# Attention and expert feed-forward on one core: output weights prepared earlier, four output tiles projected inside the last head pair

## The reference

```
x = L0_attn_x                                   # [2, 2048, 1024] f32
x = x + layernorm(attn(layernorm(x)))           # 16 heads of 64, causal, with biases
x = x + layernorm(ffn(layernorm(x)))

attn(x): q, k, v = x @ w.T + b; softmax(q k^T / 8, causal) v; @ wo.T + bo

ffn(x):  per expert n of 8:
    x_diff = x - select_mean_diff[n];  x_diff /= norm(x_diff)
    score[n] = sum_s (select_weight[n, :, s] . x_diff) ** 2
    gate[n] = sigmoid(imp_slope[n] * (score[n] - imp_center[n]))
  scale = max gate, i = argmax gate
  mod = bias_w[i] + lora_degen[i] . (lora_update[i] . (x - debias_w[i]))
  return (1 - scale) * x + scale * mod
```

## Time and profile before

| | us |
|---|---|
| three runs | 2406.46, 2402.87, 2405.65 |
| median | 2405.65 |
| span of the profiled execution | 2400.4 |
| time of the profiled execution | not given apart; the median stands 5.25 above the span |
| PE busy | 2271.6 |
| DVE, ACT, POOL busy | 1675.7, 1741.4, 1633.9 |

### The profile page before, as it was taken

The page is one execution under the profiler, slowest core; times in us unless marked ns, Lnnn a source line. Parts: engine busy times, 40 slices in busy tenths (PEclk is TensorE's granted clock), DMA queues, the critical chain, the costliest instruction groups (busy, mean ns, idle before and its releaser), DMA issues. The chain is left out here.

```text
span 2400.4 us, 70752 instructions
## 1 busy us (share of the span) xinstructions
PE 2271.6 (95%) x28666; PEld 1448.5 (60%) x28666; DVE 1675.7 (70%) x4148; ACT 1741.4 (73%) x2380; POOL 1633.9 (68%) x1291
## 2 busy tenths in 40 slices
PE   6999999999999998899999999999999679999996
PEld 4566667575757655557575757575766445455453
DVE  8487777777777766566666666666676846777777
ACT  6577777877777766677777777777787846666665
POOL 3588888888888876678788888888898822222221
PEclk9999999999999999999999999999999889999998
DMA  8699999999999999999999999999999986656662
GB/s 244 124 196 202 194 211 207 196 203 204 209 197 197 208 200 198 198 200 193 174 195 181 189 183 187 185 184 185 182 192 195 232 169 155 165 153 174 149 168 79
DMA packets 1414420, 447.44 MB, mean 186 GB/s; under 512 B 1391664, under 2 KB 1392064, under 8 KB 1414096
## 3 DMA queue, kind: packets, MB, share of 16 engines
q1 hardware_dynamic: 1414096, 442.92, 99.7%
HBM read 67.95 MB, written 41.94 MB: 46 GB/s over the span
## 5 line engine op out<-in xcount | busy, mean ns | idle before, releaser
L1051 POOL TENSOR_TENSOR hl<-probs,hl 128x1024 f16<-128x1024 f32 x544 | 1166.6, 2151 | 350.2 <-ACT hl L903 348.1
L896 ACT ACTIVATE probs<-s_ps,exp_bias 128x1024 f32<-128x1024 f32 (+7 forms) x768 | 633.3, 854 | 316.5 <-DVE exp_bias L730 309.7
L725 DVE TENSOR_REDUCE neg_max<-s_ps 128x1 f32<-128x1024 f32 (+7 forms) x768 | 675.8, 904 | 169.2 <-PE s_ps L526 169.1
L903 ACT ACTIVATE hl<-probs 128x1024 f16<-128x1024 f32 x544 | 575.0, 1057 | 90.2 <-DMA pt<-hl 74.1
L549 PE MATMUL o_ps<-v,pt 128*128 128x65 f16 x4352 | 431.1, 193 | 50.2 <-DMA pt<-hl 43.8
L549 PEld LDWEIGHTS o_ps<-v,pt 128*128 128x128 f16 x4352 | 400.5, 96 | 79.3 <-DMA pt<-hl 36.9
L526 PE MATMUL s_ps<-nat 64*128 64x512 f16 (+3 forms) x3840 | 410.1, 351 | 25.9 <-ACT probs L896 22.4
L550 PE MATMUL o_ps<-v,pt 128*128 128x65 f16 x4352 | 431.4, 194 | 0.0
L551 PE MATMUL o_ps<-v,pt 128*128 128x65 f16 x4352 | 430.2, 192 | 0.0
L550 PEld LDWEIGHTS o_ps<-v,pt 128*128 128x128 f16 x4352 | 399.8, 97 | 19.1
L551 PEld LDWEIGHTS o_ps<-v,pt 128*128 128x128 f16 x4352 | 400.3, 98 | 0.0
(11 more groups left out here) (185 smaller groups left out, 3580.9 us busy)
## 6 DMA issues: line engine op xcount, KB each, us to landing
w_raw<-in_w_pairs SPq DMA_DIRECT2D x48, 576.0 KB, 4.8
o_scratch<-o_hl SPq DMA_DIRECT2D x128, 128.0 KB, 2.6
out<-result SPq DMA_DIRECT2D x31, 512.0 KB, 3.1
x_in<-in_x SPq DMA_DIRECT2D x27, 512.0 KB, 4.9
pt<-hl SPq DMA_TRANSPOSE x544, 5.2
xn_scratch<-xn SPq DMA_DIRECT2D x16, 512.0 KB, 3.8
xn<-in_x SPq DMA_DIRECT2D x11, 512.0 KB, 3.8
x_in_c<-in_x SPq DMA_DIRECT2D x10, 512.0 KB, 3.9
```

Of the source, the lines that this page charges most:

```text
L725: nc.vector.tensor_reduce(neg_max[:, step.round, acc, h:h + 1], s_ps[(n + h) % S_RING][:, first:end], AX_X, ALU.max, negate=True).then_inc ...
L896: last = nc.scalar.activation(probs_of(n)[:, cols], s_ps[n % S_RING][:, cols], ACT.Exp, bias=exp_bias[:, step.round, acc, h:h + 1], scale= ...
L903: nc.scalar.activation(hl_of(n, 0), probs_of(n), ACT.Copy).then_inc(p_hi_done, 1)
L1051: nc.gpsimd.tensor_tensor(hl_of(n, 1), probs_of(n), hl_of(n, 0), ALU.subtract).then_inc(p_lo_done, 1)
```

## The change

Four things are changed.

1. The splitting of w_o moves out of the last pair. From step 8 of pair 8 to pair 12 one block per 8 steps (`wo_block`) is loaded into x_in (part 0), summed on ACT (1), centred on DVE (2), its high part made on ACT (3), its low part on DVE (4), and stored from xn to a new DRAM scratch (5). Both buffers are those of the norm, which is over after pair 6. In the last pair SP loads the eight finished blocks (512 KB each) into the arena in its steps 3 to 6, two per step. POOL has no part in it any more.
2. In the last pair's steps 9 to 16 PE projects one half of tiles 0 to 3 per step into u_ps, between scores and times_v (`project_early`), and DVE copies it out in the next step (`early_out`). Six `load_o` stand in SP's steps 5, 7, 9, 10, 12 and 14, the last three behind a wait for proj_done. After the last pair PE projects tile 4 instead of tile 0.
3. The last stage has six attn buffers instead of two. Its 54 halves that are left are laid out by `project_at`: steps 1 to 31 have two halves each, and steps 2, 5, ..., 23 only one. So the projection is four tiles ahead at first and back at the old place from step 24. The other work keeps its step.
4. Row loads, other loads and `center_rows` of the last pair come up to three steps earlier. nat[0] lies in the new tile attn_first.

```diff
+FIRST_WO = HALF_PAIRS * NSTEP + 8
+WO_SPAN = 8
+def wo_block(p, i, part):
+    k, at = divmod(p * NSTEP + i - FIRST_WO, WO_SPAN)
+    return k if 0 <= k < KT and at == part else None
+EARLY_TILES, EARLY_FIRST = 4, 9
+EARLY_HALVES = 2 * EARLY_TILES
...
@@ SP, body of a pair
-                    if kind == "last" and i == NSTEP - LAG:
-                        fin["load_o"](sp, 0)
-                        fin["load_x"](sp, 0)
...
-                            sp.dma_start(wo_raw[k], fin["w_view"][k]).then_inc(wo_loaded[k], 16)
...
+                    k = wo_block(p, i, 0)
+                    if k is not None:
+                        if k:
+                            sp.wait_ge(wo_lo_done, k)
+                        else:
+                            sp.wait_ge(xn_lo_done, 2 * LN_TILES)
+                        sp.dma_start(x_in[:], fin["w_view"][k]).then_inc(wo_loaded, 16)
+                    k = wo_block(p, i, 5)
+                    if k is not None:
+                        sp.wait_ge(wo_lo_done, k + 1)
+                        sp.dma_start(wo_scratch[k], xn[:]).then_inc(wo_stored, 16)
+                    if kind == "last" and 3 <= i < 3 + KT // 2:
+                        if i == 3:
+                            sp.wait_ge(unit_done, N_UNIT * PAIRS)
+                            sp.wait_ge(wo_stored, 16 * KT)
+                        for k in (2 * (i - 3), 2 * (i - 3) + 1):
+                            sp.dma_start(fin["w_pair"][:, :, k, :], wo_scratch[k].rearrange("p (l d) -> p l d", l=2)).then_inc(
+                                wo_ready[k], 16)
...
+                    if kind == "last":
+                        for tile, at in enumerate((5, 7, 9, 10, 12, 14)):
+                            if i == at:
+                                if tile >= 3:
+                                    sp.wait_ge(fin["proj_done"], 2 * (tile - 3) + 2)
+                                fin["load_o"](sp, tile)
+                        if i in (13, 15):
+                            fin["load_x"](sp, (i - 13) // 2)
@@ PE
+            def project_early(n):
+                m, h = divmod(n, 2)
+                if h == 0:
+                    pe.wait_ge(fin["ot_loaded"][m % 3], 16 * (m // 3 + 1))
+                if n == 0:
+                    pe.wait_ge(full_done, N_UNIT * PAIRS)
+                    for k in range(KT):
+                        pe.wait_ge(wo_ready[k], 16)
+                else:
+                    pe.wait_ge(fin["attn_done"], n)
+                project_half(nc, fin, m, h, u_ps[:])
...
+                    if kind == "last" and i >= EARLY_FIRST:
+                        project_early(i - EARLY_FIRST)
@@ DVE
+            def early_out(n):
+                m, h = divmod(n, 2)
+                dve.wait_ge(fin["proj_done"], n + 1)
+                dve.wait_ge(fin_centered, 1)
...
+                    if kind == "last" and i > EARLY_FIRST:
+                        early_out(i - EARLY_FIRST - 1)
@@ last stage
+ONE_HALF = range(2, 25, 3)
+def project_at():
+    halves, at = [divmod(n, 2) for n in range(EARLY_HALVES + 2, 2 * B * QT)], {}
+    for m in range(1, B * QT):
+        n = 1 if m in ONE_HALF else 2
+        at[m], halves = halves[:n], halves[n:]
...
-                if has(0) and m >= 1:
-                    project(m, 0)
+                for half in projected[m][:1]:
+                    project(*half)
...
-                if has(0):
-                    attention_out(m, 1)
+                for half in ([(EARLY_TILES, 1)] if m == 0 else projected[m][-1:]):
+                    attention_out(*half)
...
-                if has(1):
-                    attention_out(m + 1, 0)
+                for half in projected[m + 1][:-1]:
+                    attention_out(*half)
```

More of the change, by code:

```diff
@@ L287, in attend_phase @@
         rows_loaded = sem("rows_loaded")
-        wo_loaded = [sem(f"wo_loaded{k}") for k in range(KT)]
+        wo_loaded = sem("wo_loaded")
         fin_mean_done = sem("fin_mean_done")
@@ L296, in attend_phase @@
         wo_lo_done = sem("wo_lo_done")
-        wo_lo_late = sem("wo_lo_late")
+        wo_stored = sem("wo_stored")
+        wo_ready = [sem(f"wo_ready{k}") for k in range(KT)]
         x_view = x.rearrange("(b t p) d -> b t p d", b=B, p=P)
[L302 to L305, removed]
         pt_left = pt[:].rearrange("p b n -> p (b n)")
@@ L456, in body @@
                         store_rows(p - 1, 1)
[L458 to L465, removed]
-                            sp.dma_start(wo_raw[k], fin["w_view"][k]).then_inc(wo_loaded[k], 16)
-                    if kind == "last" and i == KT - 1:
-                        sp.wait_ge(unit_done, N_UNIT * PAIRS)
+                    k = wo_block(p, i, 0)
[16 more added lines that the diff above has]
+                                wo_ready[k], 16)
+                    if kind == "last" and i == 5:
                         sp.wait_ge(mix_set, 2)
@@ L838, in body @@
                 if kind == "last":
+                    early_out(EARLY_HALVES - 1)
                     output_read(p, N_ROUND - 1)
@@ L966, in body @@
                         split_weight(*split)
[L967 to L970, removed]
+                    k = wo_block(p, i, 1)
+                    if k is not None:
+                        wo_sum(k)
+                    k = wo_block(p, i, 3)
+                    if k is not None:
+                        wo_high(k)
                     for n, row in enumerate(("bo_row", "degen", "bias")):
-                        if kind == "last" and i == 11 + n:
+                        if kind == "last" and i == 8 + n:
                             row_sum(n, fin[row][:])
@@ L1121, in _ @@
             pairs(body)
+ONE_HALF = range(2, 25, 3)
[4 more added lines that the diff above has]
+        at[m], halves = halves[:n], halves[n:]
+    assert not halves
+    return at
+PROJECT_AT = project_at()
 def finish_inputs(nc, ctx, x, o_scratch, wo, b_o, ident_in, ffn_in, ffn_probe, ffn_mix, own_in, rank_in, center, slope):
@@ L1237, in finish_phase @@
         minus_half = sb("minus_half_c", [P, 1], F32)
[L1238 to L1247, removed]
-        mixed = ring(2, "mixed", [P, D], F32)
-        y = ring(2, "y", [P, D], F32)
-        result = ring(2, "result", [P, D], F32)
         attn_sum, attn_var, attn_rstd = (ring(SC, n, [P, 1], F32) for n in ("attn_sum", "attn_var", "attn_rstd"))
@@ L1267, in finish_phase @@
         mix_t = sb("mix_t", [P, 2 * P], F16)
+        ot = fin["ot"]
+        fin["x_first"].append(sb("x_in_c", [P, D], F32)[:])
+        x_in = fin["x_first"]
+        attn = [fin["attn_first"][:, i * D:(i + 1) * D] for i in range(EARLY_TILES)]
+        attn += [tile[:] for tile in ring(AT - EARLY_TILES, "attn", [P, D], F32)]
+        x1 = ring(X1, "x1_", [P, D], F32)
+        x2 = ring(X2, "x2_", [P, D], F32)
+        x2_hl = ring(2, "x2_hl", [P, 2 * D], F16)
+        x2t = ring(2, "x2t", [P, 2 * KT, P], F16)
+        square = ring(2, "square", [P, D], F32)
+        mixed = ring(2, "mixed", [P, D], F32)
+        y = ring(2, "y", [P, D], F32)
+        result = ring(2, "result", [P, D], F32)
         proj_ps = fin["proj_ps"]
@@ L1318, in finish_phase @@
         LAST = NT - 1
+        projected = [PROJECT_AT.get(m, []) for m in range(NT + 5)]
+        project_step = {half: m for m, some in enumerate(projected) for half in some}
         def last_half(h, part):
@@ L1361, in step @@
                     transpose_x2(m - 2)
+                for tile in range(EARLY_TILES + 2, NT):
+                    if m == max(project_step[tile, 0] - 2, 0):
+                        load_o(tile)
                 if has(2):
-                    load_o(m + 2)
                     load_x(m + 2)
@@ L1441, in step @@
                     nc.tensor.matmul(dots_ps[:], ones[:], own_dots[:], start=True, stop=True).then_inc(offsets_ps_done, 1)
-                if has(0) and m >= 1:
-                    project(m, 1)
+                for half in projected[m][1:]:
+                    project(*half)
                 if has(-2) and m - 2 < LAST:
@@ L1609, in step @@
                     last_residual(LAST)
-            attention_out(0, 0)
+            attention_out(EARLY_TILES, 0)
             steps(step)
```

98 lines of the change are left out of this document (44 added, 54 removed).

## The result

| | before | after |
|---|---|---|
| median of four runs, us | 2406.06 (2402.87 to 2415.34) | 2492.55 (2490.46 to 2496.21) |
| span of the profiled execution | 2400.4 | 2488.6 (its time: 2490.46) |
| up to the start of pair 8 | 1053.5 | 1057.5 |
| pairs 8 to 12 | 567.9 | 627.6 |
| pairs 13 and 14 | 212.1 | 211.0 |

Ratio 1.0356 [1.0337, 1.0375]: slower by 3.6%, where 0.7% was forecast, and outside the range. Of the 88.2 us of span, 59.6 lie in pairs 8 to 12, which the prediction had charged with 3. (Pair starts are DVE's first bias_min of each pair. The 4.0 before pair 8 lie in code that is the same; other kernels with that code start pair 8 between 1053.7 and 1058.3.)

A forecast was written before the change was run, and what follows sets the result against it. The prediction took the ring of DVE, ACT and GpSimd, not PE, to bound the last stage. Its terms, 0 - 5.4 - 1.6 + 17.5 + 3 + 4 = +17.5 us, put 2405.65 at 2423, range 2405 to 2442.

The forecast's parts named there:

- Term 5: w_o's split beside pairs 8 to 12: +3 us (0 to 7), priced from norm tiles in pairs 1 to 5.
- Term 2: Start of the last stage, up to residual 3: -5.4 us, as attn 0 to 3 already exist.
- Term 4: Last pair: +17.5 us (bounds +2 and +30), from early halves on PE and waiting for the last weights.
- Term 1: Last stage in steady state: 0 us; 28 steps of 13.15 stay, though 41.4 us of PE work leave.
- the ring: Last stage: DVE, ACT and GpSimd work from one tile's residual to the next, without PE, 13.15 us per tile.
- Rival B: PE bounds the last stage, so halves taken out give back 41.4 us: -22.5, 2383 us; chance 0.09.
- the ring without gates and y: Start of the last stage, residual 0 to 1: 9.9 us instead of 11.97, so 2.1 saved.
- Term 3: Hand-over from the last pair to the last stage: -1.6 us, 10.8 instead of 12.44, PE coming warm.
- Rival D: DMA holds the last pair, PE waiting for pt, and the clock does harm: +28, 2434 us, up to 2445; chance 0.22.
- Term 6: Clock falling in the last stage's short steps: +4 us, bounds 0 and 13.
- The base: Median 2405.65 us stands 5.25 over the 2400.4 span, taken as launch and end, untouched by the change.
- Rival C: Last pair absorbs the halves, weights there on time, term at +7.4: total +3.4, 2409 us; chance 0.17.

The follow-up runs named there:

- e2: Kernel before without the hi x w_lo matmul of each projection block, a third of the projection left out; 2400.7 us, ratio 0.997.
- e6: Kernel before with ACT's attention_squares moved behind ffn_gated in the last stage; 2397.07 us, ratio 0.9955.
- e9: e1 with nothing projected in the last pair, only the early w_o split and its DRAM scratch kept; 2418.16 us, ratio 1.0037.
- e5: e1 with the weight loads earlier in SP's last pair (three, three, two in steps 3 to 5), row loads in step 5; 2432.24 us, ratio 1.0103.
- e3: e1 with one matmul instead of 24 in each early half, tiles 0 to 3 wrong; 2422.8 us in one run.
- e11: e10 with the eight scratch loads one per step in SP's steps 3 to 10 instead of two per step; 2402.12 us, ratio 0.9976.
- e1: Changed kernel with the w_o load kept in place and all that needs it two steps later, beside pairs 8 to 12; 2434.28 us, ratio 1.0116.
- e8: e1 with PE projecting the one half of each short step twice, the second overwriting the first; 2435.21 us, ratio 1.0119.
- e10: e9 with ACT's attention_squares moved behind ffn_gated in the last stage; 2406.12 us, ratio 0.9989.

## Why the prediction was wrong

It was right that the kernel gets slower, and in the bound of the last stage. Term 5 failed in its mechanism and makes 56.6 of the 70.7 us by which the change of the span was missed (88.2, forecast 17.5); terms 2 and 4 were mis-sized, and term 4 left out a second limit.

- **Term 1 (0).** Right. e2 takes far more PE work away, with residuals still 13.16 to 13.20 apart, and e6 shortens the ring and wins. Rival B (2383) falls. PE's own pace is 12.75 (e6), not 12.93, so its slack beside the ring was 0.4 us and not 0.2. The page "Perfetto Trace Analysis" of the Trainium skill (Identifying the Most-Contended Engine) says to optimise the most-contended engine first, and warns that TensorE's matmul busy share is no good measure of how near it is to its limit. Here that share, 97%, was a fair measure (12.75 of 13.15), and still work taken off PE won nothing.
- **Term 2 (-5.4): -2.8.** e9, without the early tiles, is back at 43.36, so the gain is theirs. What failed is "the ring without gates and y": residual 0 to 1 took 12.34 us, not 9.9. In step 1 DVE's list has attention_out of tile 5 ahead of x2_low, and it waited 5.17 us for PE. I had checked that op in the short steps, not where PE was still filling its lead.
- **Term 3 (-1.6): -1.8.** Right.
- **Term 4 (+17.5): +25.4.** The steps behind the wait were right: scores to scores 8.1 us and then 6.6 (forecast 8.26 and 6.79), and 62.2 us from the first half to the pair's end (61.9). Mis-sized was when the weights are there, 78.1 us into the pair and not 70.5 (bounds 68.5 to 73.5). I took SP's slot of step 6 from the old schedule plus two transfers; the new schedule puts two loads per step, five row loads and a transpose ahead of it. But the wait is not the whole cause. e5 removes it and wins only 4.5 of 14, and e3 removes the matmuls and wins 7. The sum that the runs bear out goes over e9: 7.7 are there without any early tile, as waits for transposes (3.4 of them go when the scratch loads come one per step, e11), and 17.7 (e1 less e9) come with the halves, their o transposes and the wait for the weights. Rival D's sign, PE waiting for pt, did not appear in after (4.5 us in all, beside 14.3 for the weights), but its mechanism lies right under the forecast's: take the wait away, and the waits for pt appear.
- **Term 5 (+3, bounds 0 to 7): +59.6 in pairs 8 to 12.** The step that failed is "pairs 1 to 5 carry nearly the same". Count and size of the ops were near enough alike, as e1 confirms with a price of 2.3. Not alike was the lead from a load to its first reader. In the kernel before, the norm's load and its first reader stand so on the timelines of SP and DVE:
```profile
353.92 0.42 SPq L393 DMA_DIRECT2D x_in<-in_x  x1
...
363.58 1.28 DVE L649 BATCH_NORM_STATS2 stats_a<-x_in 128x6 f32<-128x512 f32 x2
```
9.7 us from issue to reader (5.3 to 12.0 over the sixteen tiles, and DVE waited for none of them), against a reader that is there 1.55 us *before* the issue (1307.88 and 1309.43). Term 4 used that SP runs steps late; term 5 had the same queue and I didn't ask. The prediction's "load x_in one step before use" was moreover a misreading of the old kernel: there the load of the next tile stands in SP's step 7t + 7, its first reader in DVE's step 7t + 9, which is two steps. It is the new work that has one. With 59.6 in place of 3 the sum would have been 2480.
- **Term 6 (+4): +4.8.** Near in number, and in good part by its cause: the fall of the clock makes 3.2 of the 4.8 (after less e8). Seven of the 28 tiles are longer in after, 13.48 to 15.20 us. Four of them have the 0.25 us ahead of y that e8 has too, which is 1.4 us in all and was in no term.
- **The base.** The profiled run after took 1.9 us more than its span, and the later runs of before 2.1 to 2.3. So of the 5.25 us over the span 3 were not launch and end but the difference between two runs; it doesn't touch the change.

With e1 term 5 is mended, and 2434 is what the other terms would have had to give: 11 above the forecast, of which terms 4 and 2 make 7.9 and 2.6. Rival C (last pair at most 7 us longer) falls too.

Still open: why the last pair of e11 (119.6) is still 4.7 us longer than that of before. The o transposes, the row loads and the last stage's loads stand in other steps than before, and they weren't tried apart. Open too is how the 17.7 us of the early tiles divide between the halves, the four o transposes and the wait for the weights: e3 and e5 take out one part each and the others grow.

## What to carry to other kernels

When a load is put "one step ahead", ask how far the issuing queue runs behind the reader; a row that shows the same work elsewhere is a price only if it also shows the same distance from issue to first reader. Moving the readers two steps later was enough here. An engine at 97% can stand beside the bound: follow one tile through the chain and look for an op that can leave the ring; moving one activation won 11 us where moving 41 us of matmuls won none. Filling an idle stretch is not free when what fills it comes through the queue that made the stretch idle: PE's idle time in the last pair was waiting for SP's transposes, and the weights and operands of the early tiles went through SP as well.

## What the runs showed of the hardware

The granted clock fell behind short gaps. In e2 it was 0.89 over 290 us, with 22 waits for mix of 3.7 us at most, about one per tile. In after, the step shown with PE busy 8.48 of 13.15 us ends in this wait, and the next step has 0.78:
```profile
2193.20 0.40 PE L1463 MATMUL u_ps<-ident_c,mix 128*128 128x128 f16 x2 [3.57 <-DVE mix L1603]
```
Matmuls whose result is overwritten, which fill the step, brought the stage back to 1.00 (e8). The page "TensorE: Matmul & The Clock Gate" of the Trainium skill (Why this matters for your kernels) warns of such gaps; the traces agree.

How loads are spread in front of DMA transposes matters, at the same number and size: eight 512 KB loads at one per step instead of two shortened PE's waits for pt from 31.2 us to 27.5, and the pair from 123.0 to 119.6 (e10, e11).
